# First queries copied by engines and first scores in two bank sets; first keys projected beside the norm and first scans in two bank sets

## The chip, the core and the metric

The kernel runs on one core of a Trainium2 chip as one program. The metric is the device time of one execution in microseconds (us). TensorE (PE) multiplies matrices from SBUF into PSUM, which has eight banks of 128 partitions by 512 float32. VectorE (DVE), ScalarE (ACT) and GpSimd (POOL) do elementwise work, and the queue of SyncE (SP) issues DMAs. The engines run side by side and wait for one another by semaphores only.

## The reference, cut to what matters

Four layers, each of self attention, context attention ("xattn") and a feed-forward part, all added to a residual of 4 x 256 rows of 128. The change touches the context attentions of the first two layers:

```python
def _L0_xattn_ref(x, context, Wq, Wk, Wv, Wout, bout):      # 8 heads of 128
    qh, kh, vh = ...                        # [8, b * n, 128]: the batches are joined
    sim = jnp.einsum('hid,hjd->hij', qh, kh) * SCALE
    mean = jnp.mean(sim, axis=-1, keepdims=True)
    sim = (sim - mean) * ATTN_MATRIX_SCALE + mean
    attn = jax.nn.softmax(sim, axis=-1)
    out = jnp.einsum('hij,hjd->hid', attn, vh)
    ...
    return jnp.einsum('bni,iq->bnq', out, Wout) + bout

def _L1_xattn_ref(query, key_value, Wq, bq, Wk, bk, Wv, bv, Wo, bo):   # 16 heads of 8
    q, k, v = ...                           # [4, 16, 256 or 1601, 8]
    attn = jnp.einsum('bhqd,bhkd->bhqk', q, k) * scale
    attn = jnp.clip(attn, -CLAMP, CLAMP)
    attn = jax.nn.softmax(attn, axis=-1)
    attn = jnp.where(jnp.any(jnp.isnan(attn)), 1.0 / Nkv, attn)
    return jnp.einsum('bhqk,bhkd->bqhd', attn, v).reshape(B, Nq, Cq) @ Wo + bo
```

The context is 4 x 1601 rows of 96. In layer 0 each of 1024 queries meets all 6404 rows, in layer 1 only the 1601 of its own batch.

## The kernel before, in words

The program is a row of stages. A stage gives each engine a straight list of instructions and ends in a barrier of all engines.

**Context attention of layer 0** (`attend_all_places`). The key weights are folded into the queries, so a query is a vector of 96 and is multiplied with the context itself. The work is 16 blocks (8 heads, two halves of 512 queries), each of two units (23 and 27 tiles of 128 context rows). Tiles go in groups of up to four, called slots `s`; `GROUP` lists all 208, unit 0 is slots 0 to 5, unit 1 slots 6 to 12. A slot goes this way:

- `score(s)` on PE: the 96 values are cut into three thirds of 32 (`t`), and tile `i` of the group uses the partitions 32i to 32i+31, so the queries must lie four times, once in each group of 32 partitions, three thirds each (`q_thirds`). These are twelve moves of 32x512, twelve DMAs for a block. The products fill banks 0 to 3.
- `take(s)` on ACT: two copies of two banks each to a ring of 11 slots in SBUF. `score(s + 1)` waits for both.
- `maximum`, `fold` on DVE and `partition_all_reduce` on POOL make the greatest score of a unit; nine slots later (`LAG`) `shift` on DVE subtracts it, `exponentials` on ACT follows, and ten slots later `values` on PE adds products into bank 4 or 5.
- `query(n)` makes the next block's queries in bank 7, five slots into the block's first unit; ACT copies them to `q1` and SP sends the twelve DMAs.

For slots 0 to 9 PE has scores only.

**Context attention of layer 1** (`layer1_context`). Stages: clearing buffers and sending for the first two batches' context; `normalise_columns` (norm in rows, eight turns by PE, two copies); `linear_columns` (the queries); `attend_clipped`. There are 16 units (batch b, group g of four heads). A unit's queries first meet all keys in `scan` to find the maxima: 11 bursts (`NB`) of up to three products, each reduced by DVE (`reduce_`) before the next burst may write the same banks 0 to 2. `prepare`, `turn` and `add` put the maxima into the queries; then `fill` makes the scores a second time in banks 3 to 6 in an order fixed by the list `X_SLOTS` (keys, values, floor, then pairs of tiles), ACT's `take` empties each, DVE's `clip` clips, and PE's `values` multiplies. The bursts of unit u+1 lie between the tiles of unit u. Before unit 0 all 11 bursts, and the first five of unit 1, stand alone. The keys (`k_rows`, 16 heads of 8 rows) must be spread to 32-partition groups (`kT`) by 16 DMAs; before the change this followed fill ("keys", 0) at the start of `attend_clipped`.

## Time and profile before

| | us |
|---|---|
| median of 3 runs | 4377.2 |
| lowest and highest of them | 4367.52, 4378.14 |
| the profiled execution, its own time | 4368.58 |
| its span in the trace | 4366.9 |
| PE busy in the span | 3340.7 (77%) |
| DVE busy | 2986.0 (68%) |
| ACT busy | 1871.6 (43%) |

The columns of a table of stretches are busy microseconds of each engine with the number of instructions, then the granted clock of TensorE as a share of full speed, the DMA share and GB/s. A row of the order of time has its start, how long the merged instructions took, the engine, the line, what is written from what, how many, and in brackets the idle time of the engine before it with what ended it. One float32 matmul of the program shows as two in the profile. PEld is PE's loading of weights. The layer-0 context attention runs from about 189 to 1570 us, the layer-1 one from 1740 to about 2330.

### The profile page before, as it was taken

The numbers are of one execution on the slowest core, as the hardware profiler recorded it, in microseconds if no ns is written. First come the engines' busy times: TensorE is split into PE (matmuls) and PEld (weight loads), VectorE is DVE, ScalarE is ACT, GpSimd is POOL, SyncE is SP. The second block draws the span as 40 slices with busy tenths as digits, with TensorE's granted clock in tenths as the row PEclk, the third lists the DMA queues.
The fourth block names the chain that finished last, engine by engine and source line by source line (L and its number), as shares of the span: only waits on it lengthen the run. The fifth ranks groups of instructions, "written<-read, shape, count | busy, mean of one in ns | idle before, by whom it ended". The sixth has DMA issues, their size and how long they took to land. (4 is left out here: it accounts for less than half of the span.)

```text
span 4366.9 us, 59636 instructions
## 1 busy us (share of the span) xinstructions
PE 3340.7 (77%) x24338; PEld 1728.6 (40%) x24338; DVE 2986.0 (68%) x4093; ACT 1871.6 (43%) x2165; POOL 352.6 (8%) x150
## 2 busy tenths in 40 slices
PE   6689999999999965577775886366654669577579
PEld 3433333333333323233333654222222346354357
DVE  4467777777777776498896545699998454546642
ACT  2255565556556542144443132444443235245233
POOL 0000000000000000000000000034442000000000
PEclk9799999999999978699998898565666799688789
DMA  2000000000000000000000200100000101010010
GB/s 81 16 13 11 8 8 15 8 8 15 8 8 13 3 7 18 14 14 9 9 1 15 106 2 21 27 0 0 0 0 0 40 2 39 9 39 1 1 38 8
DMA packets 22180, 69.30 MB, mean 16 GB/s; under 512 B 5393, under 2 KB 5905, under 8 KB 21010
## 3 DMA queue, kind: packets, MB, share of 16 engines
q1 hardware_dynamic: 21906, 65.47, 5.1%
q8 instruction: 193, 3.16, 0.3%
q14 instruction: 81, 0.66, 0.1%
HBM read 49.07 MB, written 0.52 MB: 11 GB/s over the span
## 5 line engine op out<-in xcount | busy, mean ns | idle before, releaser
L1050 PE MATMUL banks<-L0x_ring,L0x_context_rows 128*101 128x512 f32 x1600 | 734.7, 602 | 3.6 <-ACT L0x_ring L1096 3.6
L1106 ACT COPY L0x_ring<-banks 128x1024 f32<-128x1024 f32 (+1 forms) x416 | 387.1, 982 | 567.7 <-PE banks L1038 567.7
L1038 PE MATMUL banks<-L0x_q_thirds,L0x_context_thirds 32*128 32x512 f32 x4800 | 607.8, 617 | 28.4 <-ACT L0x_ring L1106 18.1
L1134 DVE TENSOR_TENSOR L0x_ring<-L0x_ring,L0x_greatest 128x2048 f32<-128x2048 f32 (+1 forms) x208 | 469.6, 2266 | 11.3 <-ACT L0x_ring L1106 9.7
L1150 DVE TENSOR_TENSOR L0x_maxima<-L0x_maxima,L0x_ring 128x1024 f32<-128x1024 f32 (+1 forms) x288 | 322.7, 1162 | 219.2 <-ACT L0x_ring L1106 219.2
L1050 PEld LDWEIGHTS banks<-L0x_ring,L0x_context_rows 128*101 128x101 f32 x1600 | 253.9, 167 | 455.9 <-issue 450.0
L1096 ACT ACTIVATE L0x_ring<-L0x_ring 128x2048 f32<-128x2048 f32 (+1 forms) x208 | 386.0, 1856 | 16.6 <-DVE L0x_ring L1134 16.2
L1038 PEld LDWEIGHTS banks<-L0x_q_thirds,L0x_context_thirds 32*128 32x128 f32 x4800 | 239.0, 188 | 376.8 <-issue 312.2
L1544 ACT ACTIVATE L1x_probs<-banks 128x2048 f32<-128x2048 f32 (+1 forms) x112 | 196.6, 1756 | 259.3 <-PE banks L1474 217.2
L1577 DVE TENSOR_REDUCE L1x_maxima<-banks 128x3 f32<-128x1203 f32 (+1 forms) x176 | 241.5, 1372 | 87.5 <-PE banks L1443 87.4
L1443 PE MATMUL banks<-L1x_k,L1x_q 32*128 32x401 f32 x1024 | 179.9, 586 | 120.6 <-DVE L1x_maxima L1577 105.1
L1600 DVE SCALAR_TENSOR_TENSOR L1x_probs<-L1x_probs,L1x_floor 128x1024 f32<-128x1024 f32 (+1 forms) x208 | 252.1, 1216 | 14.0 <-ACT L1x_probs L1544 14.0
L1235 POOL PARTITION_ALL_REDUCE L0x_greatest<-L0x_folded_maxima x32 | 93.8, 2930 | 1420.6 <-DVE L0x_folded_maxima L1167 728.4
L3346 PE MATMUL banks<-L2x_k,L2x_q_of_head 128*128 128x512 f32 (+1 forms) x256 | 182.4, 807 | 0.0
L3451 DVE MAX8 L2x_top<-L2x_rest 128x8 f32<-128x1601 f32 x96 | 175.6, 1829 | 3.3
L1474 PE MATMUL banks<-L1x_q_shifted,L1x_k 32*128 32x256 f32 (+1 forms) x1664 | 170.1, 399 | 5.9 <-ACT L1x_probs L1544 4.7
L3456 DVE MATCH_REPLACE8 L2x_rest<-L2x_top,L2x_rest 128x1601 f32<-128x1601 f32 x96 | 173.8, 1811 | 0.0
L1150 DVE TENSOR_TENSOR L0x_maxima<-L0x_ring 128x1024 f32<-128x1024 f32 x64 | 75.5, 1221 | 118.8 <-ACT L0x_ring L1106 118.8
L1443 PEld LDWEIGHTS banks<-L1x_k,L1x_q 32*128 32x128 f32 x1024 | 57.5, 195 | 208.6 <-DVE L1x_maxima L1577 180.6
L3419 POOL TENSOR_TENSOR L2x_exp_all<-L2x_exp_all,L2x_exp_rest 128x1601 f32<-128x1601 f32 x31 | 110.9, 3578 | 260.9 <-ACT L2x_exp_top L3409 260.9
L248 PE MATMUL banks<-identity,z_rows 128*128 128x128 f32 x96 | 25.0, 439 | 135.7 <-DVE z_rows L281 135.7
L1474 PEld LDWEIGHTS banks<-L1x_q_shifted,L1x_k 32*128 32x128 f32 (+1 forms) x1664 | 108.0, 186 | 38.3 <-ACT L1x_probs L1544 15.6
(943 smaller groups left out, 5245.5 us busy)
## 6 DMA issues: line engine op xcount, KB each, us to landing
L0x_q_thirds<-L0x_q_context SPq DMA_DIRECT2D x192, 64.0 KB, 2.0
L1f_expert_weights<-in_L1f_experts SPq DMA_DIRECT2D x16, 512.0 KB, 9.6
L2f_expert_weights<-in_L2f_experts SPq DMA_DIRECT2D x8, 512.0 KB, 5.4
L3a_expert_weights<-in_L3a_experts SPq DMA_DIRECT2D x8, 512.0 KB, 5.8
L3f_expert_weights<-in_L3f_experts SPq DMA_DIRECT2D x8, 512.0 KB, 5.9
L1x_k<-L1x_k_rows SPq DMA_DIRECT2D x64, 50.0 KB
L0x_context_thirds<-in_context_thirds SPq DMA_DIRECT2D x1, 2496.0 KB, 14.2
L1x_context<-in_context SPq DMA_DIRECT2D x4, 600.4 KB, 5.3
```

The costliest lines, as they stand in the source:

```text
L1038: mm = pe.matmul(k.ps[:, i, :], thirds[group_rows(i), slot, t, :], q_thirds[group_rows(i), u // 2 % 2, t, :], start=t == 0, stop=t == 2)
L1050: mm = pe.matmul(k.ps[0:CW, bank, :], rows1[0:height(j), j, :], ring[0:height(j), s % RING, i, :], start=s == FIRST[u] and i == 0, stop=s ...
L1096: act.activation(ring[:, s % RING, 0:len(js), :], ring[:, s % RING, 0:len(js), :], ACT.Exp).then_inc(exped, 1)
L1106: act.copy(ring[0:r, s % RING, 2 * p:2 * p + len(pair), :], k.ps[0:r, 2 * p:2 * p + len(pair), :]).then_inc(copied, 1)
L1134: dve.tensor_tensor(o, o, greatest[:, u % 2, None, :].broadcast_to([P, len(js), 512]), ALU.subtract).then_inc(shifted, 1)
L1150: dve.tensor_tensor(o, before, ring[0:r, s % RING, 2 * p:2 * p + m, :], ALU.max).then_inc(maxed, 1)
L1443: mm = pe.matmul(k.ps[:, i, 0:WIDE], qT[row(h), g, b * S + it * P:b * S + (it + 1) * P], kT[row(h), b % 2, g, 400 * c:400 * c + WIDE], sta ...
L1474: mm = pe.matmul(k.ps[0:height(j), 3 + h, i * S:(i + 1) * S], kT[row(h), b % 2, g, j * P:j * P + height(j)], qs[row(h), u % 2, :], start=T ...
L1544: act.activation(probs[0:r, at % 2, 0:m, :].rearrange("p a (h q) -> p h a q", h=4), k.ps[0:r, 3:7, 0:m * S].rearrange("p h (a q) -> p h a ...
L1577: dve.tensor_reduce(mx[:, u % 2, items[0]:items[-1] + 1], k.ps[:, 0:len(items), 0:WIDE], X, ALU.max).then_inc(reduced, 1)
L1600: dve.scalar_tensor_tensor(out=o, in0=o, scalar=1.0, in1=floor[0:height(j), u % 2, :], op0=ALU.min, op1=ALU.max).then_inc(clipped, 1)
L3346: mm = pe.matmul(k.ps[:, i, 0:m], qh[:, h, b * S + it * P:b * S + (it + 1) * P], kT[:, b % 2, c:c + m], start=False, stop=True)
```

## The change

In layer 0: block 0's queries are no longer spread by DMAs but by three copies on ACT and nine on DVE; slots 1, 3, 5 and 7 (`ALONE` = 8) write banks 4 to 7, and slots 2 to 7 wait for the copies of the slot two before; the second block's query product moves from behind slot 5 to behind slot 8. In layer 1: batch 0's keys are projected at the start of the norm's stage, placed by ACT there, and spread in two parts (groups 0 and 1 during the queries' stage, 2 and 3 at the start of the attention); unit 0's odd bursts write banks 3 to 5, and a burst waits for the reduction of the burst two before; the first values, floor and pair are made after unit 0's scans, each followed by a burst of unit 1.

```diff
@@ -240,6 +240,8 @@
 
         @block.tensor
         def _(pe):
+            if keys:
+                keys.project(pe)
...
@@ -251,6 +253,8 @@
         def _(act):
             act.wait_ge(var_ready, 1)
             act.activation(k.sd[:, 0:tiles], k.ve[:, 0:tiles], ACT.Sqrt).then_inc(sd_ready, 1)
+            if keys:
+                keys.place(act)
...
@@ -296,11 +300,16 @@
                 dve.tensor_scalar(dstT[:, middle:2 * middle], k.ps[:, 1, 0:middle], column_gain, column_shift, ALU.mult, ALU.add)
 
 
-def linear_columns(k, jobs, values=None, tiles=TILES):
+def linear_columns(k, jobs, values=None, tiles=TILES, keys=None):
 
     items = [(j, half) for j in jobs for half in range(tiles // 4)]
     with k.stage() as (block, signal):
         product, by_act, by_dve, cleared = signal(), signal(), signal(), signal()
+
+        if keys:
+            @block.sync
+            def _(sp):
+                keys.spread(sp, range(0, 2))
...
+ALONE = 8
...
+        def score_bank(s):
+            return 4 if s < ALONE and s % 2 else 0
+
+        def query_at(u):
+            return FIRST[u] + 5 if u else ALONE
+
         @block.sync
         def _(sp):
-            for n in range(BLOCKS):
+            for n in range(1, BLOCKS):
...
                 if s == FIRST[u] and u % 2 == 0:
-                    pe.wait_ge(spread, SPREAD * (u // 2 + 1))
-                if s:
+                    if u:
+                        pe.wait_ge(spread, SPREAD * (u // 2))
+                    else:
+                        pe.wait_ge(first_spread, 12)
+                if 2 <= s < ALONE:
+                    pe.wait_ge(copied, 2 * (s - 1))
+                elif s >= ALONE:
                     pe.wait_ge(copied, 2 * s)
                 slot = s - FIRST[u // 2 * 2]
                 for t in range(3):
                     for i, j in enumerate(js):
-                        mm = pe.matmul(k.ps[:, i, :], thirds[group_rows(i), slot, t, :], q_thirds[group_rows(i), u // 2 % 2, t, :],
+                        mm = pe.matmul(k.ps[:, score_bank(s) + i, :], thirds[group_rows(i), slot, t, :], q_thirds[group_rows(i), u // 2 % 2, t, :],
                                        start=t == 0, stop=t == 2)
...
-                    if s == FIRST[u] + 5 and u % 2 == 0 and u + 2 < UNITS:
+                    if s == query_at(u) and u % 2 == 0 and u + 2 < UNITS:
...
+            act.wait_ge(query_placed, 2)
+            for t in range(3):
+                act.copy(q_thirds[group_rows(0), 0, t, :], q1[group_rows(t), :]).then_inc(first_spread, 1)
...
+            dve.wait_ge(query_placed, 2)
+            for t in range(3):
+                for i in range(1, 4):
+                    dve.tensor_copy(q_thirds[group_rows(i), 0, t, :], q1[group_rows(t), :]).then_inc(first_spread, 1)
...
-X_SLOTS = [("keys", 0), ("values", 0), ("floor", 0), ("pair", 0)]
+X_SLOTS = [("values", 0), ("floor", 0), ("pair", 0)]
...
+    def project(self, pe):
+        pe.wait_ge(self.arrived[0], 16)
+        for i, (c, m) in enumerate(CHUNKS):
+            mm = pe.matmul(self.k.ps[:, 3 + i, 0:m], self.w["k"], self.context[:, 0, c:c + m], start=True, stop=True)
+        mm.then_inc(self.projected, 1)
+
+    def place(self, act):
+        act.wait_ge(self.projected, 1)
+        act.activation(self.k_rows[:], self.k.ps[:, 3:7, :].rearrange("p a n -> p (a n)")[:, 0:CTX], ACT.Identity,
+                       bias=self.w["bk"]).then_inc(self.placed, 1)
+
+    def spread(self, sp, groups):
+        d = 8
+        sp.wait_ge(self.placed, 1)
+        for g in groups:
+            for h in range(4):
+                sp.dma_start(self.kT[32 * h:32 * h + d, 0, g, :], self.k_rows[32 * g + d * h:32 * g + d * (h + 1), :]).then_inc(self.here[g], 16)
...
+        def scan_bank(m):
+            return 3 if m < NB and m % 2 else 0
...
-            spread(0)
+            first_keys.spread(sp, range(2, 4))
...
-                if g == 0 and burst == 0:
-                    pe.wait_ge(spread_keys, 16 * H * (b + 1))
+                if b == 0 and burst == 0:
+                    pe.wait_ge(first_keys.here[g], 64)
+                elif g == 0 and burst == 0:
+                    pe.wait_ge(spread_keys, 16 * H * b)
                 if burst == 0 and u:
                     pe.wait_ge(shifted, u)
-                if m:
+                if u == 0 and m >= 2:
+                    pe.wait_ge(reduced, m - 1)
+                elif u:
                     pe.wait_ge(reduced, m)
+                bank = scan_bank(m)
                 for i, item in enumerate(BURSTS[burst]):
                     it, c, h = ITEMS[item]
-                    mm = pe.matmul(k.ps[:, i, 0:WIDE], qT[row(h), g, b * S + it * P:b * S + (it + 1) * P],
+                    mm = pe.matmul(k.ps[:, bank + i, 0:WIDE], qT[row(h), g, b * S + it * P:b * S + (it + 1) * P],
                                    kT[row(h), b % 2, g, 400 * c:400 * c + WIDE], start=True, stop=True)
...
-            for slot in X_SLOTS[0:2]:
-                fill(slot)
             for m in range(NB):
                 scan(m)
             turn(0)
-            for slot in X_SLOTS[2:FIRST_SLOTS]:
+            early = [m for n in range(SCAN_FROM, 0) for m in bursts_in(n)]
+            for i, slot in enumerate(X_SLOTS[0:FIRST_SLOTS]):
                 fill(slot)
-            for n in range(SCAN_FROM, 0):
-                for m in bursts_in(n):
-                    scan(m)
+                scan(early[i])
+            for m in early[FIRST_SLOTS:]:
+                scan(m)
...
-        normalise_columns(k, k.x, k.z, k.zT)
-        linear_columns(k, [(qT[:, g, :], [(w["q"][:, g * P:(g + 1) * P], k.zT)], bq[:, g:g + 1], d ** -0.5, None) for g in range(G)])
-        attend_clipped(k, w, qT, context, c_sum, marks, limit, pick, y, arrived, bufs)
+        first_keys = FirstKeys(k, ctx, w, context, arrived, bufs[0], kT)
+        normalise_columns(k, k.x, k.z, k.zT, keys=first_keys)
+        linear_columns(k, [(qT[:, g, :], [(w["q"][:, g * P:(g + 1) * P], k.zT)], bq[:, g:g + 1], d ** -0.5, None) for g in range(G)], keys=first_keys)
+        attend_clipped(k, w, qT, context, c_sum, marks, limit, pick, y, arrived, first_keys, bufs)
```

PE at the start of the layer-0 attention, before. `bank0_signal22` is `spread`, `bank0_signal1` is `copied`; L1026 is `query`, L1038 `score`, L1050 `values`.

```order
L1026 MATMUL banks<-z_columns,L0x_folded_q 100x512
L1038 MATMUL banks<-L0x_q_thirds,L0x_context_thirds 128x512 [waits bank0_signal22]
L1038 MATMUL banks<-L0x_q_thirds,L0x_context_thirds 128x512 x11
L1038 MATMUL banks<-L0x_q_thirds,L0x_context_thirds 128x512 [waits bank0_signal1]
L1038 MATMUL banks<-L0x_q_thirds,L0x_context_thirds 128x512 x11
L1038 MATMUL banks<-L0x_q_thirds,L0x_context_thirds 128x512 [waits bank0_signal1]
L1038 MATMUL banks<-L0x_q_thirds,L0x_context_thirds 128x512 x11
```

The same place after the change, L1042 and L1059 being `query` and `score`, and `bank0_signal23` the new `first_spread`.

```order
L1042 MATMUL banks<-z_columns,L0x_folded_q 100x512
L1059 MATMUL banks<-L0x_q_thirds,L0x_context_thirds 128x512 [waits bank0_signal23]
L1059 MATMUL banks<-L0x_q_thirds,L0x_context_thirds 128x512 x23
L1059 MATMUL banks<-L0x_q_thirds,L0x_context_thirds 128x512 [waits bank0_signal1]
L1059 MATMUL banks<-L0x_q_thirds,L0x_context_thirds 128x512 x11
L1059 MATMUL banks<-L0x_q_thirds,L0x_context_thirds 128x512 [waits bank0_signal1]
L1059 MATMUL banks<-L0x_q_thirds,L0x_context_thirds 128x512 x11
```

The matmuls of slots 0 and 1 stand in a row of 24 without a wait between them. Further down the row, out of this piece, the second query product moved from behind the sixth slot to behind the ninth.

PE around the norm, the queries' product and the start of the layer-1 attention, before, without the waits: L248 turns the normed rows, L321 is the queries' product, L1492 a small product into bank 7, L1460 the keys, L1463 the values, L1443 the scans of unit 0.

```order
L248 MATMUL banks<-identity,z_rows 128x128 x8
L77 UNCONDITIONAL_BRANCH
L316 UNCONDITIONAL_BRANCH
L321 MATMUL banks<-z_columns,L_weights 128x512 x8
L77 UNCONDITIONAL_BRANCH
L1430 UNCONDITIONAL_BRANCH
L1492 MATMUL banks<-L1x_minus_max 128x256
L1460 MATMUL banks<-L1x_context,L_weights 128x512 x3
L1460 MATMUL banks<-L1x_context,L_weights 128x65
L1463 MATMUL banks<-L_weights,L1x_context 128x128 x12
L1463 MATMUL banks<-L_weights,L1x_context 65x128
L1443 MATMUL banks<-L1x_k,L1x_q 128x401 x32
```

After it (L1433 the first keys, L250, L330 and L1558 as L248, L321 and L1492, L1509 the scans, L1516 the turn of the maxima):

```order
L1433 MATMUL banks<-L1x_context,L_weights 128x512 x3
L1433 MATMUL banks<-L1x_context,L_weights 128x65
L250 MATMUL banks<-identity,z_rows 128x128 x8
L77 UNCONDITIONAL_BRANCH
L325 UNCONDITIONAL_BRANCH
L330 MATMUL banks<-z_columns,L_weights 128x512 x8
L77 UNCONDITIONAL_BRANCH
L1491 UNCONDITIONAL_BRANCH
L1558 MATMUL banks<-L1x_minus_max 128x256
L1509 MATMUL banks<-L1x_k,L1x_q 128x401 x32
L1516 MATMUL banks<-identity,L1x_minus_max 128x128 x2
L1529 MATMUL banks<-L_weights,L1x_context 128x128 x12
```

The keys' four products stand ahead of the norm's turns, the scans follow the small product at once, and the values' products (L1529) now stand behind the turn of the maxima.

ACT in the norm's stage of layer 1, before (L253 is the root, L257 the three scalings that wait for `rooted`):

```order
L250 UNCONDITIONAL_BRANCH [waits barrier_Pool_Activation_PE_DVE_SP_release]
L253 ACT_TABLE_LOAD
L253 ACTIVATE norm_sd<-norm_var_eps 128x8 [waits bank1_signal1]
L257 ACTIVATE z_rows<-x_residual,norm_sd,norm_rstd 128x128 [waits bank1_signal5]
L257 ACTIVATE z_rows<-x_residual,norm_sd,norm_rstd 128x128 x2
L261 COPY z_columns<-banks 128x512 [waits bank1_signal6]
```

After (L255, L261 in their place, L1438 the placing of the keys):

```order
L252 UNCONDITIONAL_BRANCH [waits barrier_Pool_Activation_PE_DVE_SP_release]
L255 ACT_TABLE_LOAD
L255 ACTIVATE norm_sd<-norm_var_eps 128x8 [waits bank1_signal1]
L1438 ACTIVATE L1x_k_rows<-banks,L_weights 128x1601 [waits L1x_first_keys_projected]
L261 ACTIVATE z_rows<-x_residual,norm_sd,norm_rstd 128x128 [waits bank1_signal5]
L261 ACTIVATE z_rows<-x_residual,norm_sd,norm_rstd 128x128 x2
L265 COPY z_columns<-banks 128x512 [waits bank1_signal6]
```

The placing stands between the root and the scalings.

## Rows read from the trace of the kernel before

**Rows 1.** the page: the span, which begins the page
```profile
span 4366.9 us, 59636 instructions
```
**Rows 2.** table of stretches: steady layer-0 attention; scans of unit 0; steady layer-1 attention
```profile
500.00:1000.00 500.00, 500.00 (x2486) 194.40 (x2488) 378.56 (x306) 295.07 (x257) 35.23 (x12) 1.00 0.04 10
1786.30:1800.00 13.70, 7.58 (x27) 2.55 (x30) 5.64 (x4) 0.00 (x0) 0.00 (x0) 0.50 0.00 0
2000.00:2300.00 300.00, 230.81 (x2650) 118.05 (x2650) 276.51 (x249) 134.94 (x152) 0.00 (x0) 0.99 0.03 6
```
**Rows 3.** order of time, start of the layer-0 attention
```profile
191.96 0.58 ACT L1091 COPY L0x_q_context<-banks 96x512 f32<-96x512 f32 x1
...
201.59 4.39 PE L1038 MATMUL banks<-L0x_q_thirds,L0x_context_thirds 32*128 32x512 f32 x24 [10.27 <-DMA L0x_q_thirds<-L0x_q_context]
...
206.02 1.93 ACT L1106 COPY L0x_ring<-banks 128x1024 f32<-128x1024 f32 x2 [13.48 <-PE banks L1038]
...
208.00 4.55 PE L1038 MATMUL banks<-L0x_q_thirds,L0x_context_thirds 32*128 32x512 f32 x24 [2.02 <-ACT L0x_ring L1106]
...
246.78 0.20 PEld L1038 LDWEIGHTS banks<-L0x_q_thirds,L0x_context_thirds 32*128 32x128 f32 x4 [0.22 <-issue]
247.21 0.20 PEld L1038 LDWEIGHTS banks<-L0x_q_thirds,L0x_context_thirds 32*128 32x128 f32 x4 [0.23 <-issue]
```
**Rows 4.** order of time: DVE's SBUF copy beside POOL's reduction, and without
```profile
322.56 0.78 DVE L1182 COPY L0x_first_sums<-L0x_scores_beyond 4x512 f32<-4x512 f32 x1
...
1561.47 0.42 DVE L1182 COPY L0x_first_sums<-L0x_scores_beyond 4x512 f32<-4x512 f32 x1
```
**Rows 5.** order of time: second query product, slot 8, first product with values
```profile
238.58 2.03 PE L1026 MATMUL banks<-z_columns,L0x_folded_q 128*100 128x512 f32 x2
...
251.12 4.19 PE L1038 MATMUL banks<-L0x_q_thirds,L0x_context_thirds 32*128 32x512 f32 x24 [2.01 <-ACT L0x_ring L1106]
...
266.65 3.68 PE L1050 MATMUL banks<-L0x_ring,L0x_context_rows 128*101 128x512 f32 x8
```
**Rows 6.** DMA issues of the page, then order of time around the norm of layer 1
```profile
L1x_context<-in_context SPq DMA_DIRECT2D x4, 600.4 KB, 5.3
...
1740.10 0.81 SPq L1667 DMA_DIRECT2D L1x_context<-in_context  x2
...
1749.98 1.26 ACT L257 ACTIVATE z_rows<-x_residual,norm_sd,norm_rstd 128x128 f32<-128x128 f32 x3 [1.28 <-DVE norm_sd L279]
...
1752.36 0.69 DVE L294 COPY z_columns<-banks 128x512 f32<-128x512 f32 x1 [1.13 <-PE banks L248]
```
**Rows 7.** order of time, start of the layer-1 attention
```profile
1763.69 1.82 DVE L1604 TENSOR_REDUCE L1x_context_sum<-L1x_context 96x1 f32<-96x1601 f32 x1 [1.10 <-PEq L77]
...
1764.19 2.91 PE L1460 MATMUL banks<-L1x_context,L_weights 96*128 96x512 f32 x8
...
1767.14 1.60 ACT L1527 ACTIVATE L1x_k_rows<-banks,L_weights 128x1601 f32<-128x1601 f32 x1 [3.76 <-PE banks L1460]
1768.76 10.78 SPq L1416 DMA_DIRECT2D L1x_k<-L1x_k_rows  x16
1768.79 3.16 PE L1463 MATMUL banks<-L_weights,L1x_context 96*128 96x128 f32 x26 [1.69 <-ACT L1x_k_rows L1527]
...
1783.09 1.72 PE L1443 MATMUL banks<-L1x_k,L1x_q 32*128 32x401 f32 x6 [11.13 <-DMA L1x_k<-L1x_k_rows]
1784.86 1.41 DVE L1577 TENSOR_REDUCE L1x_maxima<-banks 128x3 f32<-128x1203 f32 x1 [19.35 <-PE banks L1443]
1786.32 1.72 PE L1443 MATMUL banks<-L1x_k,L1x_q 32*128 32x401 f32 x6 [1.52 <-DVE L1x_maxima L1577]
```
**Rows 8.** order of time: last reduction, turn, first clip
```profile
1817.21 0.99 DVE L1577 TENSOR_REDUCE L1x_maxima<-banks 128x2 f32<-128x802 f32 x1 [1.81 <-PE banks L1443]
...
1818.71 0.69 PE L1450 MATMUL banks<-identity,L1x_minus_max 128*128 128x128 f32 x2 [1.55 <-DVE L1x_minus_max L1585]
...
1839.45 1.22 DVE L1600 SCALAR_TENSOR_TENSOR L1x_probs<-L1x_probs,L1x_floor 128x1024 f32<-128x1024 f32 x1
```

More of the change, by code:

```diff
@@ L223, with normalise_columns @@
 ACT_TILES = (3, 6, 7)
-def normalise_columns(k, src, rows, dstT, gain=None, shift=None, column_gain=None, column_shift=None, eps=1e-5, values=None, tiles=TILES):
+def normalise_columns(k, src, rows, dstT, gain=None, shift=None, column_gain=None, column_shift=None, eps=1e-5, values=None, tiles=TILES, keys=None):
     shared = [t for t in ACT_TILES if t < tiles] if gain is None else ()
@@ L1085, in query @@
                 act.wait_ge(queried, n + 1)
-                if n:
-                    act.wait_ge(spread, SPREAD * n)
+                if n == 1:
+                    act.wait_ge(first_spread, 12)
+                elif n:
+                    act.wait_ge(spread, SPREAD * (n - 1))
                 if n >= 3:
@@ L1105, in take @@
                     r = height(pair[-1])
-                    act.copy(ring[0:r, s % RING, 2 * p:2 * p + len(pair), :], k.ps[0:r, 2 * p:2 * p + len(pair), :]).then_inc(copied, 1)
+                    bank = score_bank(s) + 2 * p
+                    act.copy(ring[0:r, s % RING, 2 * p:2 * p + len(pair), :], k.ps[0:r, bank:bank + len(pair), :]).then_inc(copied, 1)
             def weigh(n):
@@ L1119, in _ @@
                 for u in range(UNITS):
-                    if s == FIRST[u] + 5 and u % 2 == 0 and u + 2 < UNITS:
+                    if s == query_at(u) and u % 2 == 0 and u + 2 < UNITS:
                         query(u // 2 + 1)
@@ L1388, with __init__, attend_clipped @@
 SLOT = {slot: n for n, slot in enumerate(X_SLOTS)}
-def attend_clipped(k, w, qT, context, c_sum, marks, limit, pick, y, arrived, bufs):
+class FirstKeys:
+    def __init__(self, k, ctx, w, context, arrived, k_rows, kT):
+        self.k, self.w, self.context, self.arrived, self.k_rows, self.kT = k, w, context, arrived, k_rows, kT
+        self.projected, self.placed = (ctx.enter_context(k.nc.semaphore("L1x_first_keys_" + n)) for n in ("projected", "placed"))
+        self.here = [ctx.enter_context(k.nc.semaphore(f"L1x_first_keys_{g}_spread")) for g in range(4)]
+    def project(self, pe):
[13 more added lines that the diff above has]
+                sp.dma_start(self.kT[32 * h:32 * h + d, 0, g, :], self.k_rows[32 * g + d * h:32 * g + d * (h + 1), :]).then_inc(self.here[g], 16)
+def attend_clipped(k, w, qT, context, c_sum, marks, limit, pick, y, arrived, first_keys, bufs):
     d, H, G = 8, 16, 4
@@ L1524, in take @@
                 if kind == "keys":
-                    if at:
-                        act.wait_ge(spread_keys, 16 * H * at)
+                    for g in range(G):
+                        act.wait_ge(first_keys.here[g], 64)
+                    if at > 1:
+                        act.wait_ge(spread_keys, 16 * H * (at - 1))
                     act.activation(k_rows[:], k.ps[:, 3:7, :].rearrange("p a n -> p (a n)")[:, 0:CTX], ACT.Identity, bias=w["bk"]).then_inc(taken, 1)
@@ L1576, in reduce_ @@
                 dve.wait_ge(scanned, m + 1)
-                dve.tensor_reduce(mx[:, u % 2, items[0]:items[-1] + 1], k.ps[:, 0:len(items), 0:WIDE], X, ALU.max).then_inc(reduced, 1)
+                dve.tensor_reduce(mx[:, u % 2, items[0]:items[-1] + 1], k.ps[:, scan_bank(m):scan_bank(m) + len(items), 0:WIDE], X, ALU.max).then_inc(reduced, 1)
             def prepare(u):
```

2 lines of the change are left out of this document (1 added, 1 removed).

## The prediction

> **What bounds the kernel now.** Read first the page's header [rows 1]: one span of 4366.9 us on one core; the run that it belongs to took 4368.58 us, so 1.7 us lie outside the span and the sum below is made against 4368.6. The change touches two places of a long chain of stages, so the shares of the whole say little. The next view is the table of stretches [rows 2]. From 500 to 1000 us, inside the first context attention, TensorE (PE) is busy for all 500 us at a granted clock of 1.00 and VectorE (DVE) for 379 us: once that stage runs, PE bounds it, and every microsecond by which its steady part begins earlier is a microsecond of the kernel. From 2000 to 2300 us, inside the second attention, it is DVE: 276.5 of 300 us. There too an earlier beginning is kept. The third view is the order of time at both beginnings. In the first one PE waits for twelve DMAs until 201.59, and then before every group of scores about 2.0 us for ScalarE's (ACT's) copies [rows 3]. In the second one PE waits until 1783.09 for the DMAs that spread the keys [rows 7], and then PE's scans and DVE's reductions take strict turns, 3.23 us a burst (1783.09 to 1786.32).
>
> **First attention: the spread of the first queries.** ACT has the queries in SBUF at 191.96 + 0.58 = 192.54 [rows 3]. Twelve DMAs then needed until 201.59. Now ACT makes three copies and DVE nine, of 32x512 each, SBUF to SBUF. The nearest rows for DVE are its copy of 4x512: 0.42 us with GpSimd (POOL) idle, 0.78 us with POOL reducing [rows 4]; POOL is idle at 192 us. The next instruction begins 0.04 us behind it at best, so nine are 9 x 0.46 = 4.1 us, and 9 x 0.82 = 7.4 us at the dear end. ACT's three, at the 0.58 of its own copy of 512 columns, are 1.8 us beside them. With 0.1 us of hand-over PE starts at 196.8 (bounds 196.0, if neighbouring copies overlap by a tenth of a microsecond each, and 200.0). Gain 4.8 us, bounds 1.6 and 5.6.
> Here the Trainium skill bears on the price: "VectorE: DVE Perf Modes", section "Two Vector instructions with no wait between them", says that an instruction whose output starts in another group of 32 partitions than the last one's is held until every earlier one is finished. The nine outputs go round groups 1, 2, 3, so each would be held and the sum stays 4.1 us; without the rule it would be 3.3. No row of before has such a series, so this is not shown here.
>
> **First attention: scores in two sets of banks.** Slots 0 to 7 now alternate between banks 0 to 3 and 4 to 7, and slot s waits for the copies of slot s-2. A slot's matmuls took 4.55 us where PE had just waited. At full clock a group of four weight loads follows the last every 0.43 us (246.78 to 247.21), and a slot has six: 2.58 us. ACT's two copies take 1.93 us, less than that, so PE no longer waits for them; DVE's maxima are further behind but free no bank of PE. So: slot 0 from 196.8, 4.39 us as before, because PE comes from idleness; seven slots of 2.58 = 18.1; then slot 8 goes back to bank 0 and waits for slot 7's copies, 2.0 us. Slot 8 begins at 221.3, against 251.12 [rows 5]: 29.8 us earlier, 4.8 of them from the spread. If a slot is worth 2.86 (the length that the profile gives to a whole group at full clock), it is 27.8.
> The second query's product (2.03 us at 238.58) moves from behind slot 5 to behind slot 8, since bank 7 is used until then. On PE it falls into the 2.0 us in which slot 9 waits for copies, so it costs 0 to 0.5. On ACT its two copies (1.2 us) stand behind slot 8's and are done before slot 9's scores. SP's twelve DMAs start then, and slot 13 needs them: five slots later, over 20 us, against the 9 us which twelve DMAs needed before. Hidden; if not, the wait is single and at most 9 us. From slot 8 to the first product with the values 15.5 us passed (251.12 to 266.65), and the same program stands there; those three slots ran at mixed clock, so -3 to +2. The chain that frees this product (maxima of slots 0 to 5, POOL, subtraction, exponential) has the whole of slots 6 to 9 in it and is not last. I take **-29 us** for this attention, between -22 and -33.
>
> **Second attention: the first keys beside the norm.** The context was sent for at 1740.10 and lands 5.3 us later [rows 6], so at 1745.4 to 1746.4 PE may project it. That took 2.91 us at clock 1.0 [rows 7]; PE has been idle, so I take up to twice that, 4 to 5.5 us: done at about 1750.9. ACT must then place the rows (1.60), and only behind that stand its three scalings (1.26), which before began at 1749.98. They now end near 1753.8; the last turn and DVE's copy (0.69) follow, 1754.8 against 1752.36 + 0.69 = 1753.05. So the norm is **1.8 us longer** (0.5 to 3.4): this is the price of the edit. Eight of the sixteen spreading DMAs go out under the queries' product: at 10.78 / 16 = 0.67 us each that is 5.4 us of a stage of 10 us; the others follow at the attention's start, for units 2 and 3, a hundred us before they are wanted. The product itself may find a warmer PE (0 to -2 us).
>
> **Second attention: scans in two sets.** Its stage starts 1.8 us later. PE's small product, then at once scan 0 follow, where before stood the keys' projection, the placing, and the wait until 1783.09. DVE's context sum (1763.69, 1.82 us) now ends at 1767.3 and is the last thing that the first reduction waits for. Then eleven reductions. One takes 1.41, and 1.46 with the hand-over (1784.86 + 1.41 against PE's start at 1786.32). With two sets a scan has a reduction's time to be ready. At the lower clock it needs 1.72, a little more than 1.46, and the turn is 1.63 us (half of 1.72 + 1.41 + two hand-overs); at the higher one DVE never waits. Ten at 1.46 and a last one of 0.99: 15.6 us, the end at 1782.9; with 1.63, at 1784.6. Before it was 1817.21 + 0.99 = 1818.20 [rows 8]. Gain 35.3 or 33.6; I take 34.5.
> Behind it the values' product (3.16 us at clock 1.0, up to 6.3 at the lower level) now stands on PE ahead of the next unit's first scan; floor and first pair stand between the next scans and run for the most part under DVE's reductions. Before, floor, exponential and pair stood in a row ahead of that scan, and the first clip came at 1839.45, 21.25 us behind the last reduction. By the same addition now: the turn of the maxima ends 1.2 us behind the last reduction (1818.71 + 0.69), then values 3.2, a scan of 1.7, four turns of 3.23 = 12.9 and the last reduction of 1.4: 20.4. At the lower clock the values add up to 3 more. I take +1 against before. Second attention: **-33.5 us**, between -27 and -38.
>
> **Sum.** -29 - 33.5 = -62.5, so 4368.6 - 62.5 = 4306 for an execution like the profiled one. The three timed runs lie from 4367.52 to 4378.14 with the median at 4377.2, 8.6 above the profiled one; which end the new median takes I can't know from three, and I put it between 4306 and 4315: **4310 us**.
>
> **The rivals.**
> 1. The clock stays low in the dense beginnings. For it: the stretch with scans alone stands at 0.50 [rows 2], and scores behind a wait took 4.55 a slot. At half the clock a slot is 5.16, and 7 x 2.58 = 18 us are lost. Against: slot 7 ran at full clock right behind a wait (its weight loads 0.43 us apart at 246.78 [rows 3]), and continuous work holds 1.00 [rows 2]. Gain then 44: 4325 to 4334.
> The Trainium skill, "TensorE: Matmul & The Clock Gate", section "HAM oscillation — how this bites in real kernels", says that a PE which idles shortly between groups of matmuls keeps falling back; that speaks for such a result in the scans of the second attention, where PE still pauses. By it the scans run at 1.63, by full clock at 1.46: 1.7 us in the sum, and 0.50 in the row of before agrees with it.
> 2. One of the two parts gives nothing: the first product with values of the first attention is set by another chain (maxima, POOL, subtraction), or the second's clip is. For the first: DVE does fold 0 and POOL's reduction meanwhile. Against: slot 5's copies are done near 216, and the subtraction stands on DVE behind slot 8's maxima, near 229; the chain would have to need more than those 13 us. Gain 33: 4336 to 4344.
> 3. Slower than before: the steady part of the first attention changes its rhythm. There are 208 slots; PE is full there, and if the new phase between ACT, DVE and PE left PE waiting, every slot would pay. From 62.5 / 208 = 0.30 us a slot the gain is gone, and at 0.45 the time is 4368.6 - 62.5 + 93.6 = 4400. For it: nothing but that the phase is new. Against: the program there is the same and DVE and ACT have a quarter of their time free.
> 4. It doesn't do what it says: spread copies wait for something else, or the scans for keys 0. Eight DMAs in a 10 us stage leave 2 to 3 us until they are wanted; a late landing costs at most 3 us, inside the range.
>
> **Chances.** Forecast (gain 50 to 71 before the median's place is counted) 0.84; rival 1 0.07; rival 2 0.05; rival 3 0.02; 0.02 for a loss of the gain by unseen waits that ends near no change. 0.3% is 13 us, about what a measurement tells from no change. Faster 0.96, same 0.02, slower 0.02. The range for 8 in 10: low end 4368.6 - 71 = 4298; high end 4368.6 - 51 + 8.6 = 4326.
>
> **What would show it.** First score matmul about 4.3 us behind the queries' copy, with DVE copies of 0.42; slots 1 to 7 without waits at 2.6 to 2.9 us; slot 8 near 221. Norm stage 1 to 3 us longer, ACT's placing ahead of its scalings. First scan near 1764 + 2 - 29 = 1737 on the new clock of the trace, reductions 1.46 to 1.63 apart, the first clip about 21 us behind the last of them. Wrong: slots of 5 us, copies of 0.8, a wait for a spread ahead of scan 0, or steady stretches in which PE is not at 100%.

## The result and the profile after

The changed kernel takes 4303.95 us (median of 4, 4300.98 to 4308.91) against 4377.67 for the kernel before in the same comparison. The ratio is 0.9839, 95% interval 0.9823 to 0.9855; on another chip it was 0.9846, 0.9833 to 0.986. It is faster by 1.6%. The prediction said 4310, from 4298 to 4326. (The profiled execution of the kernel before, 4368.58 us, lies near the fast end of that kernel's times, so the medians differ by 73.7 us and the two traces by 65.9.) The profiled execution's span is 4301.0 us, 65.9 less than before [rows 1].

The head of the page after:

```profile
span 4301.0 us, 59641 instructions
PE 3334.1 (78%) x24338; PEld 1735.1 (40%) x24338; DVE 2990.1 (70%) x4102; ACT 1872.6 (44%) x2168; POOL 352.4 (8%) x150
```

TensorE (PE) is busy 6.6 us less, which is clock and not work: the matmuls are as many as before. Nearly all of the gain is idle time that is gone.

Order of time after, start of the layer-0 attention (answers to [rows 3, 5]):

```profile
189.59 2.00 PE L1042 MATMUL banks<-z_columns,L0x_folded_q 128*100 128x512 f32 x2 [2.56 <-PEq L77]
...
192.84 1.90 ACT L1140 COPY L0x_q_thirds<-L0x_q_context 32x512 f32<-32x512 f32 x3
192.84 4.01 DVE L1236 COPY L0x_q_thirds<-L0x_q_context 32x512 f32<-32x512 f32 x9 [3.55 <-ACT L0x_q_context L1114]
196.91 22.55 PE L1059 MATMUL banks<-L0x_q_thirds,L0x_context_thirds 32*128 32x512 f32 x186 [5.32 <-DVE L0x_q_thirds L1236]
...
221.48 2.86 PE L1059 MATMUL banks<-L0x_q_thirds,L0x_context_thirds 32*128 32x512 f32 x24 [2.03 <-ACT L0x_ring L1130]
224.27 1.10 PE L1042 MATMUL banks<-z_columns,L0x_folded_q 128*100 128x512 f32 x2
...
234.45 3.68 PE L1071 MATMUL banks<-L0x_ring,L0x_context_rows 128*101 128x512 f32 x8 [0.37 <-ACT L0x_ring L1119]
```

Nine copies on VectorE (DVE) take 4.01 us. Slots 0 to 7 are one row of 186 matmuls without a wait: 22.55 us. The first product with the values comes 44.86 us behind the first query product (234.45 - 189.59); before it was 266.65 - 189.32 = 77.33.

Order of time after, around the norm of layer 1 (answers to [rows 6, 7]):

```profile
1707.93 0.81 SPq L1734 DMA_DIRECT2D L1x_context<-in_context  x2
...
1713.77 5.78 PE L1433 MATMUL banks<-L1x_context,L_weights 96*128 96x512 f32 x8 [7.65 <-PEq L77]
...
1719.59 1.60 ACT L1438 ACTIVATE L1x_k_rows<-banks,L_weights 128x1601 f32<-128x1601 f32 x1 [3.05 <-PE banks L1433]
1721.08 1.25 ACT L261 ACTIVATE z_rows<-x_residual,norm_sd,norm_rstd 128x128 f32<-128x128 f32 x3
...
1722.98 0.69 DVE L298 COPY z_columns<-banks 128x512 f32<-128x512 f32 x1 [3.92 <-PE banks L250]
1723.93 16.18 SPq L1446 DMA_DIRECT2D L1x_k<-L1x_k_rows  x16
1723.98 9.84 PE L330 MATMUL banks<-z_columns,L_weights 128*128 128x512 f32 x16 [1.03 <-PEq L77]
...
1734.85 1.82 DVE L1671 TENSOR_REDUCE L1x_context_sum<-L1x_context 96x1 f32<-96x1601 f32 x1 [1.10 <-PEq L77]
```

The order of time then shows the scans (answers to [rows 7, 8]); PE's row of 46 matmuls begins with the fourth scan, and two of eleven reductions stand for the rest:

```profile
1739.36 12.74 PE L1509 MATMUL banks<-L1x_k,L1x_q 32*128 32x401 f32 x46 [0.37 <-DVE L1x_maxima L1644]
...
1742.44 1.41 DVE L1644 TENSOR_REDUCE L1x_maxima<-banks 128x3 f32<-128x1203 f32 x1 [0.24 <-PE banks L1509]
...
1744.03 1.41 DVE L1644 TENSOR_REDUCE L1x_maxima<-banks 128x3 f32<-128x1203 f32 x1 [0.18 <-PE banks L1509]
...
1752.14 0.99 DVE L1644 TENSOR_REDUCE L1x_maxima<-banks 128x2 f32<-128x802 f32 x1 [0.23 <-PE banks L1509]
...
1754.12 5.75 PE L1529 MATMUL banks<-L_weights,L1x_context 96*128 96x128 f32 x26
...
1774.68 1.21 DVE L1667 SCALAR_TENSOR_TENSOR L1x_probs<-L1x_probs,L1x_floor 128x1024 f32<-128x1024 f32 x1
```

Stretches after: slots 0 to 7; the keys' product; the queries' product; the scans; of these the part from 1740.70 on; the values' product. The column ahead of the last two is the granted clock.

```profile
196.90:219.50 22.60, 22.55 (x186) 11.66 (x186) 13.19 (x12) 13.06 (x14) 0.16 (x1) 0.92 0.00 1
1713.70:1719.40 5.70, 5.63 (x9) 2.57 (x10) 4.78 (x28) 1.49 (x2) 0.00 (x0) 0.50 0.01 1
1723.98:1733.90 9.92, 9.84 (x16) 4.00 (x16) 3.00 (x4) 2.11 (x4) 0.00 (x0) 0.72 0.28 41
1735.40:1753.00 17.60, 15.35 (x65) 4.87 (x64) 15.96 (x12) 0.00 (x0) 8.54 (x4) 0.62 0.16 25
1740.70:1752.10 11.40, 11.39 (x43) 3.54 (x40) 9.88 (x7) 0.00 (x0) 3.25 (x2) 0.50 0.03 4
1754.10:1759.80 5.70, 5.70 (x28) 5.37 (x26) 0.42 (x1) 0.00 (x0) 0.00 (x0) 0.50 0.00 0
```

Where the 65.9 us are, by four marks of each trace (a: first query product; b: first product with the values; c: the two context DMAs of layer 1; d: first clip):

| | a to b | b to c | c to d | d to the end |
|---|---|---|---|---|
| before | 77.33 | 1473.45 | 99.35 | 2527.45 |
| after | 44.86 | 1473.48 | 66.75 | 2526.32 |
| difference | -32.47 | +0.03 | -32.60 | -1.13 |

The steady part of the layer-0 attention kept every microsecond. (The start a differs by 0.27 us.)

The 44.86 from a to b is the best of six. In five other profiles with the same changed attention of layer 0 this stretch took 46.31 to 46.48 us, because slot 10 ran at the lower clock; the row of one of them:

```profile
231.75 4.55 PE L1059 MATMUL banks<-L0x_q_thirds,L0x_context_thirds 32*128 32x512 f32 x24 [2.01 <-ACT L0x_ring L1130]
```

So the attention of layer 0 is worth 31 us in most executions, and some 1.5 of the 32.47 us are luck.

### The profile page after: what moved, and what is told of

It is laid out like the page before. It is cut to its first block and busy times, and to the rows that moved or that the text cites. A ratio compares the mean times of both kernels' runs of the same rounds, so it can differ in the third digit from the quotient of the medians.

```text
span 4301.0 us, 59641 instructions
## 1 busy us (share of the span) xinstructions
PE 3334.1 (78%) x24338; PEld 1735.1 (40%) x24338; DVE 2990.1 (70%) x4102; ACT 1872.6 (44%) x2168; POOL 352.4 (8%) x150
## 3 DMA queue, kind: packets, MB, share of 16 engines
q8 instruction: 193, 3.16, 0.3%
## 5 line engine op out<-in xcount | busy, mean ns | idle before, releaser
L1059 PE MATMUL banks<-L0x_q_thirds,L0x_context_thirds 32*128 32x512 f32 x4800 | 593.8, 606 | 10.3 <-DVE L0x_q_thirds L1236 5.3
L1059 PEld LDWEIGHTS banks<-L0x_q_thirds,L0x_context_thirds 32*128 32x128 f32 x4800 | 237.1, 185 | 347.0 <-issue 306.7
L1509 PE MATMUL banks<-L1x_k,L1x_q 32*128 32x401 f32 x1024 | 176.8, 579 | 92.2 <-DVE L1x_maxima L1644 87.7
L1509 PEld LDWEIGHTS banks<-L1x_k,L1x_q 32*128 32x128 f32 x1024 | 56.8, 193 | 176.0 <-DVE L1x_maxima L1644 158.6
L250 PE MATMUL banks<-identity,z_rows 128*128 128x128 f32 x96 | 25.1, 438 | 125.1 <-DVE z_rows L285 123.7
## 6 DMA issues: line engine op xcount, KB each, us to landing
L0x_context_thirds<-in_context_thirds SPq DMA_DIRECT2D x1, 2496.0 KB, 14.3
```

The lines of the kernel that those rows point to most:

```text
L1059: mm = pe.matmul(k.ps[:, score_bank(s) + i, :], thirds[group_rows(i), slot, t, :], q_thirds[group_rows(i), u // 2 % 2, t, :], start=t == 0 ...
L1509: mm = pe.matmul(k.ps[:, bank + i, 0:WIDE], qT[row(h), g, b * S + it * P:b * S + (it + 1) * P], kT[row(h), b % 2, g, 400 * c:400 * c + WID ...
```

## The experiments

Marks are as in the table. Times of single executions of one program vary by 10 to 12 us, so what is compared below are stretches between marks, except where a ratio is given.

**First attention alone, second attention alone.** The first is the kernel before with the changed `attend_all_places`; the second is the changed kernel with both edits of layer 0 undone.

> The kernel before with the changed layer-0 attention alone. Theory (each beginning gives about half, and both are kept to the end): the first product with the values comes 32.2 us earlier than before (234.45 against 266.65 us) and the time is 4368.6 to 4377.7 less 32 to 33, so 4336 to 4345, ratio about 0.9925. Rival (only one attention gives the gain, the other's loss is made up by a shift of the clock): below 4310 or above 4360.

> The changed layer-1 attention alone; the layer-0 attention as before. Theory: the first clip stands 66.75 us behind the clearing stage's start instead of 99.35, so 32.6 us less in all: 4336 to 4345, ratio about 0.9925, and the two ratios multiply to 0.984 to 0.985. Rival: the sum of the two alone is more or less than the whole by over 10 us, since one beginning takes part of its gain from the other.

Measured: 4340.58 us, ratio 0.9915 (0.99 to 0.993), and 4339.8 us, 0.9919 (0.9902 to 0.9935). Their product is 0.9835, the whole's ratio 0.9839. The first alone has a to b 46.39, b to c 1473.1 and c to d 99.0; the second alone 76.79 and 66.2. Each is half, neither touches the other's stretch.

**First queries by DMA again.**

```diff
-            for n in range(1, BLOCKS):
+            for n in range(BLOCKS):
...
-                act.copy(q_thirds[group_rows(0), 0, t, :], q1[group_rows(t), :]).then_inc(first_spread, 1)
...
-                    dve.tensor_copy(q_thirds[group_rows(i), 0, t, :], q1[group_rows(t), :]).then_inc(first_spread, 1)
```

> The changed kernel with the first queries of layer 0 again spread by twelve DMAs; two sets of banks stay. Theory: first score matmul 4.7 us later (9.05 us behind the end of ACT's query copy instead of 4.1), slots 1 to 7 still 2.58 us apart, slot 8 and everything behind it 4.7 to 5 us later, so 4307 to 4313. Rival (the engine copies matter for the clock too: PE idles 9 us before the scores and slot 0 runs slower): 6 us or more.

Measured: the first score matmul comes 12.28 us behind the query product against 7.32, so 4.96 later, but a to b is 52.73, 7.9 more than in the changed kernel's first profile, and the time is 4316.67 us, above the 4307 to 4313 of the theory. The order of time of that run:

```profile
204.98 23.77 PE L1056 MATMUL banks<-L0x_q_thirds,L0x_context_thirds 32*128 32x512 f32 x186 [10.27 <-DMA L0x_q_thirds<-L0x_q_context]
230.77 4.55 PE L1056 MATMUL banks<-L0x_q_thirds,L0x_context_thirds 32*128 32x512 f32 x24 [2.02 <-ACT L0x_ring L1125]
```

The eight slots took 1.2 us more and slot 8 ran 4.55 instead of 2.86 us. But the five other profiles with the changed first attention had 46.3 to 46.5 from a to b, so against them it is 6.3 more. 5 us of later start are shown. Whether the longer idleness ahead of slot 0 costs clock as well, as the rival has it, one run doesn't tell: behind the same idle 10.27 us slot 0 took 4.39 us in the kernel before and 5.50 in the run with the second attention alone.

**One set of banks for the first scores.**

```diff
-            return 4 if s < ALONE and s % 2 else 0
+            return 0
...
-            return FIRST[u] + 5 if u else ALONE
+            return FIRST[u] + 5
...
-                if 2 <= s < ALONE:
-                    pe.wait_ge(copied, 2 * (s - 1))
-                elif s >= ALONE:
+                if s:
                     pe.wait_ge(copied, 2 * s)
```

> The changed kernel with slots 0 to 7 in banks 0 to 3 alone, each waiting for the copies of the last, and the second query product behind slot 5; the engine copies stay. Theory: slots 6.3 to 6.6 us apart again, 4.55 us of matmuls and 2.0 of waiting, first product with the values 27 us later (about 261.5), time 4329 to 4336. Rival (the engine copies gave more than their 4.7): less than 20 us later.

Measured: a to b 72.88, 28.0 more than in the changed kernel's first profile and 26.4 more than in the five others; 4334.9 us. Both as the theory had it.

**Two sets of banks, but in turn.** As the changed kernel with only the third hunk above.

> The changed kernel, slots 0 to 7 in two sets of banks as changed, but each slot waits for the copies of the last one again. Theory (the gain is the overlap and the clock that follows from it, not the banks): slots 6.3 to 6.6 us apart, from the query product to the first product with values 71 to 75 us against 44.9, time 4328 to 4338. Rival (ACT reading the banks that PE is about to write slowed both): slots below 5.5 us apart.

Measured: a to b 73.14, slots 6.57 us apart; the time, 4343.11 us, is 5 above the range named, while the stretch from d to the end, which the edit doesn't touch, took 2536.6 us, 10.3 more than in the changed kernel's profile. The second set of banks alone is worth nothing: 73.14 against 72.88.

```profile
206.08 4.55 PE L1057 MATMUL banks<-L0x_q_thirds,L0x_context_thirds 32*128 32x512 f32 x24 [2.02 <-ACT L0x_ring L1128]
212.65 4.55 PE L1057 MATMUL banks<-L0x_q_thirds,L0x_context_thirds 32*128 32x512 f32 x24 [2.01 <-ACT L0x_ring L1128]
```

**One set of banks, PE kept busy in the waits.** As the run with one set for the scores, and besides:

```diff
                 if s < len(GROUP):
                     score(s)
+                if s < 8:
+                    for _ in range(2):
+                        pe.matmul(k.ps[:, 6, :], k.ident[:], k.zT[:, 0:512], start=True, stop=True)
```

> One set of banks and the wait for the last slot's copies, as in the run with one set, but behind each of slots 0 to 7 PE makes two more products of 128x512 into the unused bank 6, whose result nobody reads; they fill most of the 2.0 us wait. Theory (of the 27 to 28 us that the second set is worth, about half is waiting and half is the lower clock after each wait): once the clock is up, slots take 2.86 + 2.0 = 4.87 us each instead of 6.56, and the first product with values comes about 10 to 14 us earlier than with one set alone, 59 to 63 us behind the query product against 72.9. Rival (the clock is given by the scores alone, waits have no part in it): 72 us or more, since the added products only cost.

Order of time of this run:

```profile
205.05 1.98 PE L1092 MATMUL banks<-z_columns,identity 128*128 128x512 f32 x4
205.16 1.93 ACT L1131 COPY L0x_ring<-banks 128x1024 f32<-128x1024 f32 x2 [2.94 <-PE banks L1057]
207.14 2.86 PE L1057 MATMUL banks<-L0x_q_thirds,L0x_context_thirds 32*128 32x512 f32 x24
209.93 1.99 PE L1092 MATMUL banks<-z_columns,identity 128*128 128x512 f32 x4
```

And the same stretch of time with one set alone, then with PE kept busy:

```profile
200.00:230.00 30.00, 20.61 (x114) 7.28 (x108) 7.36 (x7) 9.03 (x10) 0.00 (x0) 0.74 0.00 1
```

```profile
200.00:230.00 30.00, 29.48 (x168) 11.16 (x164) 13.18 (x12) 12.30 (x14) 0.36 (x1) 1.00 0.01 2
```

A slot needs 4.87 us from start to start (202.27 to 207.14) instead of 6.56, with the same waits for ScalarE's (ACT's) copies; the time is 4322.79 us and a to b is 63.64, 9.2 less than with one set alone. The theory had said 10 to 14; of its 59 to 63 the measured 63.64 just misses. Useless work made this stretch 9 us shorter: 5.9 of them up to the start of slot 8, and 3.4 behind it, where no product was added and more slots ran at full clock. So of the 26.4 to 28.0 us that overlapping is worth, about 9.2 are clock that the waits had cost (one run each, with a spread of 1.6 us). The rest holds the seven waits of 2.0 us (14), and was not split further.

**One set of banks for the first scans.**

```diff
-            return 3 if m < NB and m % 2 else 0
+            return 0
...
-                if u == 0 and m >= 2:
-                    pe.wait_ge(reduced, m - 1)
-                elif u:
+                if m:
                     pe.wait_ge(reduced, m)
```

> The changed kernel with unit 0's scans of layer 1 in banks 0 to 2 alone, each after the last one's reduction; keys beside the norm stay. Theory: reductions 3.23 us apart instead of 1.62, first clip 83 us behind the start of the clearing stage's DMAs instead of 66.8, so 16 us later: 4319 to 4326 by that difference to the changed kernel's 4303. If PE's clock is up in the scans (0.95 us each instead of 1.72): 2.5 us apart and 9 us later.

Measured: reductions 3.24 us apart, and the last is done 15.5 to 16.0 us later; the time is 4317.93 us, a little below the 4319 to 4326 expected; but c to d is 79.51, only 12.8 to 13.3 more than in the changed kernel's two profiles. From the gathering of the maxima to the first clip it took 18.8 us against 21.5: 2.7 were given back behind the scans, where the values' product took 4.80 us instead of 5.75 and the next scans 0.95 instead of 1.72, so at a higher clock. The gain of the second set is 13 and not the 16 expected.

```profile
1742.27 1.71 PE L1507 MATMUL banks<-L1x_k,L1x_q 32*128 32x401 f32 x6 [1.52 <-DVE L1x_maxima L1642]
1744.05 1.41 DVE L1642 TENSOR_REDUCE L1x_maxima<-banks 128x3 f32<-128x1203 f32 x1 [1.83 <-PE banks L1507]
...
1745.51 1.71 PE L1507 MATMUL banks<-L1x_k,L1x_q 32*128 32x401 f32 x6 [1.53 <-DVE L1x_maxima L1642]
```

**First keys at the start of the attention.** The norm and the queries' stage go without the keys; the attention begins with

```diff
+            first_keys.project(pe)
             for m in range(NB):
                 scan(m)
...
-            first_keys.spread(sp, range(2, 4))
+            first_keys.spread(sp, range(0, 4))
...
+            first_keys.place(act)
```

> The changed kernel with the first keys' product, placing and all sixteen DMAs at the start of the layer-1 attention; two sets of banks for the scans and the wait for one group's four DMAs stay, the values' product stays behind the scans. Theory: the norm's stage is 2.8 us shorter again; the small product comes 3.3 us earlier, but scan 0 waits for 2.9 of product, 1.6 of placing, four DMAs of 0.67 and their landing of about 2 us, so it starts 32.5 to 35 us behind the clearing stage's DMAs instead of 27.55, and the whole is 5 to 7 us slower. So of the 18.7 us between the two starts of scan 0 about two thirds came from no longer waiting for all sixteen DMAs and the values' product, not from the place beside the norm. Rival (it is the place beside the norm that matters): 12 us slower or more.

Measured: 4314.19 us; scan 0 stands 34.27 us behind c (before 42.99, changed 27.0 to 27.6), c to d is 72.36, 5.6 to 6.2 more than changed, as the theory had it. The two starts of scan 0, before and changed, are 15.5 to 16.0 us apart (the 18.7 of the expectation is in no row). Of these, 8.7 come from waiting for one group's four DMAs: from the first issue to scan 0 it took 14.33 us before (1768.76 to 1783.09) and 5.67 here. The values' product gone from its front gave nothing: before, it was done at 1771.95, and PE then waited 11.13 us for the DMAs. The other 6.7 to 7.3 us come from the place beside the norm: nearer half and half than the two thirds expected.

```profile
1741.91 8.12 SPq L1446 DMA_DIRECT2D L1x_k<-L1x_k_rows  x12
...
1747.58 3.04 PE L1509 MATMUL banks<-L1x_k,L1x_q 32*128 32x401 f32 x12 [7.33 <-DMA L1x_k<-L1x_k_rows]
```

**Further steps the same way.** The changed kernel again on one chip with three variants: `ALONE = 10`; the values' product between scans 0 and 1; and both of these with ACT's placing behind its scalings.

```diff
-ALONE = 8
+ALONE = 10
...
-            return 3 if m < NB and m % 2 else 0
+            return 3 if 2 <= m < NB and m % 2 == 0 else 0
...
+            scan(0)
+            fill(X_SLOTS[0])
+            for m in range(1, NB):
...
-            if keys:
-                keys.place(act)
             if shared:
                 act.wait_ge(rooted, 1)
             for t in shared:
...
+            if keys:
+                keys.place(act)
             act.wait_ge(turned, near)
```

> The changed kernel itself, as the measure for the next three on the same chip. Theory: ratio to the kernel before 0.983 to 0.985, 4300 to 4309; 44.9 to 46.4 us from the query product to the first product with values, first clip 66.2 to 66.8 us behind the clearing stage's DMAs. Rival (its first times were a lucky state of the clock): above 4315.

> Two sets of banks for slots 0 to 9 instead of 0 to 7, the second query product behind slot 10. Theory: two more waits of 2.0 and 1.0 us go and one of 2.0 stays, the first product with values comes 2.5 to 4 us earlier, 41 to 42.5 us behind the query product at a full clock. Rival (from here the chain of maxima, subtraction and exponential sets that product): 0 to 1 us.

> The values' product of layer 1 stands between scan 0 and scan 1, where PE is at full clock and DVE still busy with the context's sum, instead of behind the turn of the maxima, where it took 5.75 us at the lower clock; the even bursts from 2 on use banks 3 to 5. Theory: the scans end 2 to 3 us later, and the five following bursts begin 5 us earlier, so the first clip comes 2 to 3 us earlier, 63.5 to 64.5 us behind the clearing stage's DMAs. Rival (the product's place doesn't matter, since it is hidden by DVE): 66 us or more.

> Both of these, and ACT's placing of the keys behind the three scalings of the norm instead of ahead of them (about 1.5 us off the norm's stage, whose last copy then ends 13.8 to 14.3 us behind the clearing stage's DMAs instead of 15.3 to 15.8). Theory: 6 to 9 us less than the changed kernel on the same chip, 4292 to 4300, ratio to before 0.981 to 0.983. Rival (clock phases later on take it back): within 3 us of the changed kernel.

| | time, us | a to b | scan 0 behind c | c to d |
|---|---|---|---|---|
| changed again | 4306.1 (median of 4) | 46.47 | 26.98 | 66.19 |
| ten slots | 4304.42 (one) | 42.73 | 27.02 | 66.24 |
| values early | 4311.03 (one) | 46.31 | 27.60 | 63.74 |
| all three | 4298.87 (median of 5) | 42.64 | 22.41 | 58.90 |

Each stretch moved as expected (ten slots by 2.1 to 3.7 us, 0.2 short of the stretch named; values early by 2.4 to 3.0). The single times of the two middle rows don't show it, being within the spread. All three together: ratio 0.9826 (0.9813 to 0.984) against 0.9846 (0.9833 to 0.986), 7 us less in the median, both stretches together 11 us shorter. The two intervals overlap, but the slowest of its five times, 4301.03, lies below the fastest of the changed kernel's four, 4302.45; with the stretches that makes it the faster one. From d to the end it took 2530.3 us against 2526.1, so some 4 of the 11 us were not kept in the profiled execution; the spread of this stretch is as large.

The norm of all three shows where the placing had cost more than its own time. Its order of time:

```profile
1717.73 1.27 ACT L259 ACTIVATE z_rows<-x_residual,norm_sd,norm_rstd 128x128 f32<-128x128 f32 x3 [1.28 <-DVE norm_sd L283]
1718.95 1.04 PE L250 MATMUL banks<-identity,z_rows 128*128 128x128 f32 x8
1719.15 1.60 ACT L1438 ACTIVATE L1x_k_rows<-banks,L_weights 128x1601 f32<-128x1601 f32 x1 [0.16 <-PE banks L1433]
...
1721.52 7.11 PE L330 MATMUL banks<-z_columns,L_weights 128*128 128x512 f32 x16 [1.52 <-PEq L77]
```

DVE's copy there ends 12.9 us behind c, earlier than the 13.8 to 14.3 expected. The turns follow the keys' product at once and take 1.04 us together, and the queries' product takes 7.11 us instead of 9.84, at full clock where it had 0.72:

```profile
1721.52:1728.60 7.08, 7.08 (x16) 2.92 (x16) 3.00 (x4) 2.06 (x3) 0.00 (x0) 1.00 0.39 58
```

PE came to it without the 1.43 us wait for ACT's scalings; that this is why the clock was up is likely but not shown.

## Why the prediction was right, point by point

- *Spread of the first queries, 4.1 us of copies, PE at 196.8*: 4.01 us, PE at 196.91. Behind the query product's start PE begins 7.32 us later against 12.27 before: 4.95 saved for 4.8. Nine copies in 4.01 us are 0.446 each, and one lasted 0.42, against 0.46 for full duration plus hand-over and 0.37 for overlapping neighbours. The Trainium skill's rule on held instructions ("VectorE: DVE Perf Modes", "Two Vector instructions with no wait between them") had the first of these: the trace agrees, with 0.446 us. No run has copies that stay in one group, so the rule itself isn't tested.
- *Slots of 2.58 us, slot 8 at 221.3*: eight slots took 22.55 us against 22.5 worked out, slot 8 started at 221.48. The run that kept PE busy shows the part of the clock in it, and the run in turn that banks alone do nothing.
- *15.5 us from slot 8 to the first product with values, -3 to +2*: 12.97, since these slots ran at full clock and the query product fell into a wait, as it was said. So the layer-0 attention gave -32.5 for -29, inside its -22 to -33, and this term is most of the deviation. In the five other executions of the same stage about 1.5 us of it is missing. The chain of maxima, subtraction and exponential, which the prediction held not to be last, was last here by a little: PE waited 0.37 us for ACT's exponential. In the five others PE came to the product without idle time.
- *Norm's stage 1.8 us longer*: 2.8 (15.74 against 12.95 from c to the end of DVE's copy). The term that was too small is the keys' product, taken as 4 to 5.5 us and done at 1750.9 on the old clock of the trace; it took 5.78, at a clock of 0.50 to the end. The queries' product was expected 0 to 2 us shorter and took 9.84 against 9.30. Together scan 0 comes 1.5 us later than worked out.
- *Reductions 1.46 to 1.63 apart, 15.6 to 17.3 us for eleven*: 16.5 (1736.59 to 1753.13). From 1740.80 on they stand 1.59 to 1.65 apart at a granted clock of 0.50, as the 1.63 had it; the first three, ahead of the fall of the clock near 1740.7, took 4.03 us together, less than the 1.46 each. The reason given for the low level isn't borne out. The prediction drew on the Trainium skill's "TensorE: Matmul & The Clock Gate", "HAM oscillation — how this bites in real kernels", which tells of a PE that falls back behind waits for DMAs of several microseconds. Here the idle times were 0.97 and 0.37 us, both ahead of the fall, and in the 11.4 us at 0.50 the profile shows PE busy for 11.39. So the trace doesn't agree that pauses keep the clock low, unless short ones hide under the ends of the matmuls, which the profile only models; the cause stays open.
- *First clip 21 us behind the last reduction, +1 against before*: 21.55 against 21.25. The values' product took 5.75 us at the lower level against 3.16 before, which the prediction had allowed for, and DVE's reductions did not hide it: moved forward it saved 2.4 to 3.0 us.
- *Rivals*: no slow clock in the dense slots of layer 0 (0.92 with the first slot in it), but in layer 1 rival 1 was right in part: the keys' product, most scans and the values' product ran at 0.50; b to c unchanged, so no change of rhythm; no wait for a spread ahead of scan 0; both halves carried. The sum was -62.5 and the trace shows -65.9: 3.5 more from layer 0, 0.9 less from layer 1, and 1.1 behind the first clip, where nothing was changed, less 0.3 by which a came later. The number 4310 came within 6.1 us of the median: 3.4 are this larger gain, and 2.7 that the new median lies only 1.3 us above its profiled execution, where 4 were added. So the mechanism and its terms held, while how near the number came is in part luck.

## What to carry to other kernels

Where an engine alternates with another at the start of a stage that it later fills, a second buffer there is worth the waits and the clock that the waits cost. What layer 0 gained was still there 1473 us later: b to c took 1473.1 to 1473.7 us in thirteen of fourteen profiles (1475.7 in the other). Look in such a wait for what it really needs: four DMAs and not sixteen, which was 8.7 us. And what is slipped into an earlier stage belongs behind the work that its stage's end waits for, even on the engine that seems idle.

## What the runs showed of the hardware

- PE's clock fell and rose within a slot: with one set of banks, slots 1 to 3 took 4.55 us each behind waits of 2.0 us, and with the waits filled by unused products 2.86 us, granted clock 1.00 against 0.74 for the same 30 us. Not every such wait costs it: slots 8 and 10 of the changed kernel took 2.86 us behind 2.03 and 2.01. The two levels are 1.2 and 2.4 GHz.
- The keys' product stayed at 0.50 for all its 5.78 us of unbroken work behind 7.65 us of idleness (5.41 and 5.44 us at 0.54 in two other executions), and the queries' product behind it went at 0.72 (1.00 in the run of all three), while slot 0 behind 5.3 us of idleness came up within its 4.5 us. Which of them rises, and when, differed between executions of the same program: a to b 44.86 and 46.47.
- The first query product (a), up to which all kernels are the same, stood at 187.6 to 193.6 us in the fourteen profiles, and the rest behind d, the same in all, took 2526 to 2537 us. Most of the spread of the times lies in these two stretches; an edit worth 3 us must be read from its stretch.
